# The first two tiles in another order on every queue: mixing tables made from 24 stacked rows, low parts on VectorE, small transfers behind the taps

## The chip, the core and the metric

The kernel runs on one NeuronCore of a Trainium2 chip. The core has five engines with queues of their own: TensorE (PE, matrix products; its weight loads are shown as PEld), VectorE (DVE), ScalarE (ACT), GpSimd (POOL) and SyncE (SP, which here only issues transfers). ACT and POOL issue transfers too. Each queue is worked off in order, and the queues wait for each other through semaphores. The metric is the device time in microseconds (us) of the whole program.

## The reference

Four residual layers over `x`, which is 64 samples x 32 channels x 512 features in float32: `x = x + ffn(cond(x))`. What matters here is the first layer and the small network beside it:

```python
# layer 0: grouped convolution along the features, 9 taps, plus a bias from the condition;
# then a base matrix 512x512 and a mixture of 28 rank-8 experts, 2 of them chosen per row
c0 = conv(x, weight) + (c @ c_weight.T)[:, :, None] + bias
y0 = c0 @ base_W.T + lora(c0, top2(softmax(c0 @ gate_W.T)))
x1 = x + y0
# layers 1, 2, 3: the conditioning is a 32x32 matrix and a bias for each of the 64 samples
h   = gelu(gelu(cond @ W0 + b0) @ W1 + b1)
att = softmax(h @ W2 + b2)                     # 64 x 8
agg_w = einsum('bk,koi->boi', att, weight)     # 64 x 1024, from a table of 8 rows
agg_b = att @ bias_k                           # 64 x 32
cond(x) = agg_w @ x + agg_b
# layer 1 ffn: 8-bit fake quantisation of rows and of w, product 512x512
# layer 2 ffn: silu(x @ Wg) * (x @ Wu) @ Wd;  layer 3 ffn: 3 experts, 2 of them chosen per sample
```

## The kernel before, in words

The 2048 rows are 16 tiles of 128 rows (4 samples each). **Stage one** does layers 0 and 1 tile by tile, **stage two** layer 2 in four groups of four tiles, beside which the conditioning and the router of layer 3 run, and **stage three** the experts of layer 3. No scheduler sets the order: for each engine the program is written out by hand, one function `step(t)` for each tile in each engine's block, and the order of the calls in it is the order of the queue.

To keep float32 accuracy, an operand is split in a high part of type float32r (names in `h`) and the rest, also float32r (names in `l`), and a product is the sum of three: high x high, high x low, low x high. ScalarE makes the high parts, and VectorE or GpSimd subtract for the low ones.

On TensorE a step of stage one is: `router(t)` (L1771, 12 matmuls with `gah`/`gal`: gate logits and the low-rank inputs), `conv(t+1)` (L1705, 9 matmuls), `base(t)` (L1771, 12 matmuls with `w0h`/`w0l`), `positions(t+1)` (L1716, 4 transposes), `hidden(t)` (L1799, 2 transposes), `mix1(t-1)` (L1821, 3 matmuls with `bd1h`/`bd1l`: the conditioning of layer 1), `linear1(t-2)` and `lora(t)` (L1809, 6 matmuls with `lbh`/`lbl`). In the first two steps more is put between: `scores` (L1744), `mixing_weights` (L1751: `att` transposed; L1756: the bias part) and three times `mixed(l)` (L1763 and L1764: the table of layer l, 64 x 1024 from 8 rows of `mixw`, in plain float32), and in step 1 `weights_t` (L1850, 16 transposes of the quantised weight `wq_rows`).

Each `mixed(l)` is copied out of the banks by ScalarE (`aggs`, L896 to L898), stored to DRAM by SP (L364) and read back in another layout as `ag1` (L373) and `bcol` (L374). From `ag1` GpSimd builds the block diagonal `bd1f` (L509, which waits for `d_tab`), ScalarE its high part (L915), GpSimd its low part (L527), and then `mix1` can run.

The preamble, ahead of step 0, loads weights from SP's queue in a written order, and TensorE runs 20 matmuls on a tile of ones (`junk`, L1722), whose result nobody reads.

The granted clock of TensorE has two levels, 1.2 and 2.4 GHz; in the profile's columns they are 0.50 and 1.00.

## Time and profile before

| | us |
|---|---|
| median of 3 runs | 761.42 (760.94 to 766.59) |
| profiled execution, its own time | 761.69 |
| span of the profiled execution | 760.0 |
| busy time of PE / DVE / ACT / POOL | 742.8 / 454.8 / 301.4 / 349.8 |
| mean granted TensorE clock | 0.990 |

The span is the time from the first to the last instruction; 1.69 us of the profiled execution lie outside of it. TensorE is busy for 98% of the span, and the chain that ended last lies on it for 86%. The busy time hides two things: a matmul at half clock counts as busy for twice as long, and a matmul that is there only to set up a table counts like any other. So the first 47 us have to be read piece by piece, which the rows further down do.

### The profile page before, as it was taken

Reading aid. Unit: us, or ns where it says so; the run is one execution under the profiler, and the core shown is the slowest. Engines: PE = TensorE matmul, PEld = TensorE weight load, DVE = VectorE, ACT = ScalarE, POOL = GpSimd, SP = SyncE. Lnnn points to the kernel's source line nnn. Section 1 sums busy time; section 2 is a strip of 40 time slices with the busy share of each in tenths; the row PEclk is TensorE's granted clock in tenths of the full one; section 3 lists DMA queues with packets and bytes.
Section 4 is the critical chain, followed back from the end, with each engine's and each line's share of the span. In section 5 each row is a group of like instructions: output and inputs, shape, how many; then the busy total and the mean of one; then the engine's idle time right before and its main releaser. Section 6 shows DMA issues by size and latency. Waiting matters only on the chain.

```text
span 760.0 us, 11094 instructions
## 1 busy us (share of the span) xinstructions
PE 742.8 (98%) x3588; PEld 598.4 (79%) x3604; DVE 454.8 (60%) x1047; ACT 301.4 (40%) x578; POOL 349.8 (46%) x381
## 2 busy tenths in 40 slices
PE   8999999999899999999999999998999999999997
PEld 5588887776688888888888888877788887888886
DVE  2566776668623244773567445886578788555443
ACT  6444444443532334243434334231454354434331
POOL 2756667766435613120221015868454645554540
PEclk9799999999999999999999999999999999999999
DMA  9447455634132102210211102423512212221200
GB/s 282 78 84 186 163 168 169 185 119 153 43 138 85 54 0 86 110 28 1 84 61 51 29 24 73 168 57 110 182 43 98 84 43 61 67 79 48 70 28 28
DMA packets 45255, 68.82 MB, mean 91 GB/s; under 512 B 21784, under 2 KB 22040, under 8 KB 44936
## 3 DMA queue, kind: packets, MB, share of 16 engines
q1 hardware_dynamic: 35440, 37.87, 17.0%
q0 software_dynamic: 9152, 29.69, 12.7%
q8 instruction: 31, 0.51, 0.3%
q10 hardware_dynamic: 608, 0.55, 0.2%
q14 instruction: 24, 0.20, 0.1%
HBM read 44.94 MB, written 17.66 MB: 82 GB/s over the span
## 4 chain that ended last, share of the span: by engine, by line
PE 86%; DVE 10%; ACT 2%; issue 2%; DVEq 0%; ACTq 0%
PE bank L2101 24%; PE bank L1957 11%; PE bank L2052 11%; PE bank L2084 11%; PE bank L1771 8%; PE bank L1705 4%; PE bank L1809 3%; PE bank L2063 2%; PE bank L1841 1%; DVE junk L1410 1%; PE bank L1977 1%; PE bank L1821 1%; PE bank L1917 1%; PE bank L1722 1%; PE bank L1716 1%
## 5 line engine op out<-in xcount | busy, mean ns | idle before, releaser
L1562 DVE TENSOR_TENSOR sil<-bank,sil 128x512 f32<-128x512 f32 x56 | 38.6, 690 | 98.0 <-PE bank L2101 98.0
L2101 PE MATMUL bank<-th,wgr 128*128 128x512 f32 x224 | 88.8, 396 | 1.9 <-POOL tl L570 1.8
L2101 PE MATMUL bank<-th,wur 128*128 128x512 f32 x224 | 88.0, 393 | 0.0
L2101 PE MATMUL bank<-tl,wgr 128*128 128x512 f32 x224 | 87.8, 392 | 0.0
L2101 PE MATMUL bank<-tl,wur 128*128 128x512 f32 x224 | 87.7, 391 | 0.0
L1957 PE MATMUL bank<-wda,hh 128*128 128x512 f32 x224 | 87.5, 391 | 0.0
L1957 PE MATMUL bank<-wda,hl 128*128 128x512 f32 x224 | 87.2, 389 | 0.0
L2052 PE MATMUL bank<-wda,xch 128*128 (+1 forms) x272 | 84.5, 392 | 1.8 <-DVE xcl L1588 1.8
L1075 ACT ACTIVATE hh<-sil 128x512 fp32r<-128x512 f32 x56 | 35.4, 632 | 116.7 <-DVE sil L1562 116.7
L1067 ACT ACTIVATE sil<-bank 128x512 f32<-128x512 f32 x56 | 33.4, 597 | 96.7 <-PE bank L2101 96.6
L1564 DVE TENSOR_TENSOR hl<-sil,hh 128x512 fp32r<-128x512 f32 x56 | 45.2, 808 | 39.1 <-ACT hh L1075 39.1
L2052 PEld LDWEIGHTS bank<-wda,xch 128*128 128x128 f32 x272 | 50.6, 188 | 12.5 <-issue 2.3
L1602 DVE TENSOR_TENSOR sil<-bank,b1c 128x512 f32<-128x512 f32 x34 | 23.5, 691 | 58.0 <-PE bank L2052 54.0
L2084 PE MATMUL bank<-wgr,hth 128*128 (+1 forms) x136 | 56.1, 412 | 0.0
L2084 PE MATMUL bank<-wgr,htl 128*128 (+1 forms) x136 | 53.3, 392 | 0.0
L2052 PE MATMUL bank<-wda,xcl 128*128 (+1 forms) x136 | 53.1, 390 | 0.0
L2084 PE MATMUL bank<-wur,hth 128*128 (+1 forms) x136 | 53.0, 390 | 0.0
L2101 PEld LDWEIGHTS bank<-th,wgr 128*128 128x128 f32 x224 | 42.2, 188 | 11.9 <-issue 1.8
L793 POOL TENSOR_TENSOR raw<-raw,prod 128x512 f32<-128x512 f32 x32 | 43.0, 1343 | 18.4 <-ACT prod L1141 10.3
L509 POOL TENSOR_TENSOR bdf<-ag,mask 128x128 f32<-128x128 f32 x32 | 15.2, 506 | 77.0 <-PE bank L1917 58.7
L798 POOL DMA_INDIRECT out_dram<-ob,idx x15 | 15.7, 1047 | 75.3 <-DVE ob L1650 75.3
L2101 PEld LDWEIGHTS bank<-th,wur 128*128 128x128 f32 x224 | 42.5, 190 | 9.1
(347 smaller groups left out, 1806.0 us busy)
## 6 DMA issues: line engine op xcount, KB each, us to landing
tap<-in_x_taps_dram SPq DMA_DIRECT2D x16, 260.0 KB, 2.9
xin<-in_x_rows_dram SPq DMA_DIRECT2D x16, 256.0 KB, 2.9
xd<-xo SPq DMA_DIRECT2D x16, 256.0 KB, 3.2
xc<-xd SPq DMA_DIRECT2D x16, 256.0 KB, 3.9
xres<-xd SPq DMA_DIRECT2D x4, 1024.0 KB, 5.5
xd<-xres SPq DMA_DIRECT2D x4, 1024.0 KB, 5.2
tsd<-tf SPq DMA_DIRECT2D x4, 1024.0 KB, 4.4
raw<-in_w_dram POOLq DMA_DIRECT2D x16, 256.0 KB, 3.0
```

The costliest lines, as they stand in the source:

```text
L793: nc.gpsimd.tensor_tensor(xgb[:, t % 2], xgb[:, t % 2], prods[n - first_], ALU.add).then_inc(ch_xb, 1)
L1067: nc.scalar.activation(sil[:, m % 2], p_pre[2 * m % 3][:], ACT.Silu).then_inc(s_sil, 1)
L1075: nc.scalar.activation(hh[:, m % HSLOTS], hf[:, m % 2], ACT.Copy).then_inc(s_hh, 1)
L1562: v.tensor_tensor(hf[:, m % 2], p_pre[(2 * m + 1) % 3][:], sil[:, m % 2], ALU.mult).then_inc(s_hf, 1)
L1564: v.tensor_tensor(hl[:, m % HSLOTS], hf[:, m % 2], hh[:, m % HSLOTS].bitcast(F32), ALU.subtract).then_inc(s_hl, 1)
L1602: v.tensor_tensor(s1[:, p % 2], bank[(p + 1) % 2][:], b1c[:, bass.ds(at, D)] if kind in "AB" else b1c[:, at:at + D], ALU.add).then_inc(s_s ...
L1705: last = mm(p_cv[:].rearrange("p (b n) -> p b n", b=BPT), w, x, start=(n == 0), stop=(n == 3 * SHIFTS - 1))
L1771: last = mm(dst, x[:, k], w[:, k, :], start=(n == 0), stop=(stop and n == 3 * PH - 1), skip_group_check=True)
L1957: last = mm(p_acc[j][:], h[:, m % HSLOTS, j * P:(j + 1) * P], wda[:, m * D:(m + 1) * D], start=(m == 0 and n == 0), stop=(m == MT - 1 and ...
L2052: last = mm(bank[(p + 1) % 2][:], x, y, start=(k == 0 and n == 0), stop=(k == KT - 1 and n == 2))
L2084: last = mm(out_, x, y, start=(begins and k == 0 and n == 0), stop=(ends and k == FT - 1 and n == 2))
L2101: last = mm(p_pre[(2 * m + b) % 3][:], w[:, (m * KT + kt) * P:(m * KT + kt + 1) * P], x[:, kt], start=(kt == 0 and n == 0), stop=(kt == KT ...
```

## The change

All of it concerns the first two tiles and what precedes them; from tile 2 on every engine's `step` issues the same instructions in the same order, apart from SP, whose transfers of the tables and of the scales `swb` sit at other places among the loads.

- **The tables.** `mixw` and `mixb` (8 rows, float32) are gone. The weights and the bias columns of a layer are one table of 8 x 1056 numbers, loaded as 64 rows of 3 x 132 (`mixr`). GpSimd makes its high part `mixh`, VectorE its low part `mixl`, and three transfers from GpSimd's queue stack them into `mix3`: 24 rows, high, low, high. VectorE makes `att3` from the softmax: high, high, low. One float32r matmul over 24 rows then gives the three products at once, and `mixed(l)` is three matmuls of 396, 396 and 264 columns. The separate bias part is gone.
- **Order.** On TensorE `base(0)` comes ahead of `mixing_weights` and waits for each quarter of `w0l` by itself; `mixed(0)` comes behind `positions(1)`, `mixed(1)` and `mixed(2)` on the two sides of `conv(2)`; `weights_t` comes behind `mix1(0)`. The first block of junk has 15 matmuls for 20. ACT, DVE, POOL and SP have written-out orders for tiles 0 and 1 to match.
- **Who does what.** VectorE makes `lbl` and `wq_rows`, which GpSimd made. GpSimd keeps the four multiplications of `w1_raw`.
- **Transfers.** `conv_raw` is loaded from ACT's queue, ahead of its other loads. `bcol` is read behind the four `ag` reads of a table, and `diag_tile(0)` waits for the four alone. `tap(3)` goes ahead of the tables, `tap(4)` and `xin(2)` ahead of the scales, and the broadcast `swb` moves to n = 2 of SP's loop.

```diff
@@ SP
             load_tap(0)
-            sp.dma_start(conv_raw[:], conv_w).then_inc(d_conv, 16)
...
             sp.dma_start(ga_raw[:], l0_ga).then_inc(d_ga, 16)
+            sp.dma_start(mixr[:], mix_w).then_inc(d_mix, 16)
             sp.dma_start(w0_raw[:], l0_w).then_inc(d_w0, 16)
-            sp.dma_start(mixw[:], mix_w).then_inc(d_mix, 16)
-            sp.dma_start(mixb[:], mix_b).then_inc(d_mix, 16)
             load_tap(1)
...
+            load_tap(3)
             store_agg(0)
-            load_tap(3)
             tables(0)
             store_agg(1)
             store_agg(2)
+            load_tap(4)
+            load_xin(2)
             sp.wait_ge(s_sw, 1)
             sp.dma_start(swd.rearrange("k p -> p k"), wsc[:, 1, :], allow_slow_non_contiguous=True).then_inc(d_sw, 16)
-            sp.wait_ge(d_sw, 16)
-            sp.dma_start(swb[:], swd.rearrange("k p -> (k p)").partition_broadcast(P)).then_inc(d_swb, 16)
...
+                if n == 2:
+                    sp.wait_ge(d_sw, 16)
+                    sp.dma_start(swb[:], swd.rearrange("k p -> (k p)").partition_broadcast(P)).then_inc(d_swb, 16)
@@ POOL
             tap_lo(0)
+            def stack_rows(r, part):
+                pool.dma_start(mix3[r * MIX:(r + 1) * MIX].rearrange("k c l n -> k c (l n)"),
+                               part.rearrange("q l n -> q (l n)")).then_inc(d_mst, 16)
+            pool.wait_ge(d_mix, 16)
+            nc.gpsimd.tensor_scalar(mixh[:], mixr[:], 1.0, 1.0, ALU.mult, ALU.mult).then_inc(s_mix, 1)
+            pool.wait_ge(s_mix, 1)
+            stack_rows(0, mixh[:])
+            stack_rows(2, mixh[:])
+            pool.wait_ge(s_mix, 2)
+            stack_rows(1, mixl[:])
             tap_lo(1)
...
@@ DVE
+            w0_lo(0)
+            w0_lo(1)
+            softmax_one()
+            gating(0, None)
+            softmax_two()
+            w0_lo(2)
+            w0_lo(3)
+            gated(0)
+            dve.wait_ge(s_lbs, 1)
+            v.tensor_tensor(lbl[:], lb_raw[:], lbh[:].bitcast(F32), ALU.subtract).then_inc(s_lbs, 1)
+            hidden_lo(0)
+            t0_lo(1)
             weight_scales()
@@ PE
-            keep_busy(20)
+            keep_busy(15)
...
             def mixed(l):
 
+                pe.wait_ge(d_mst, 48)
+                pe.wait_ge(s_atc, 2)
                 if l > 0:
                     pe.wait_ge(s_agc, 3 * l)
-                mm(bank[5][0:BATCH, :], attt[:, l], mixw[:, l, 0:512], start=True, stop=True)
-                mm(bank[6][0:BATCH, :], attt[:, l], mixw[:, l, 512:AGW], start=True, stop=True).then_inc(s_ag, 1)
+                for dst, c0, c1_ in ((bank[5], 0, 3), (bank[6], 3, 6), (bank[4], 6, 8)):
+                    last = mm(dst[0:BATCH, 0:(c1_ - c0) * MIXC].rearrange("b (c n) -> b c n", n=MIXC), attt[:, l],
+                              mix3[:, c0:c1_, l], start=True, stop=True)
+                last.then_inc(s_att, 1)
```

On TensorE in step 0 the order behind `conv(1)` was this (first the program of before, from the transposes of the softmax weights on; `cvf`, `hm` and `hts` are the inputs of `positions`, `hidden` and `lora`):

```order
L1751 MATMUL bank<-ident,att 8x64 [waits s_at]
L1751 MATMUL bank<-ident,att 8x64 x2
L1756 MATMUL bank<-mixb,attt 64x32 [waits s_atc,d_mix]
L1756 MATMUL bank<-mixb,attt 64x32 x2
L1763 MATMUL bank<-mixw,attt 64x512
L1764 MATMUL bank<-mixw,attt 64x512
L1771 MATMUL bank<-w0h,t0h 128x512 [waits s_w0l]
```

and is now, from the last quarter of `base(0)` on:

```order
L1829 MATMUL bank<-w0h,t0h 128x512 [waits s_w0l]
L1829 MATMUL bank<-w0l,t0h 128x512
L1829 MATMUL bank<-w0h,t0l 128x512
L1807 MATMUL bank<-ident,att 24x64 [waits s_at]
L1807 MATMUL bank<-ident,att 24x64 x2
L1772 MATMUL bank<-ident,cvf 128x4x32 [waits s1_t0l,s1_cvs]
L1772 MATMUL bank<-ident,cvf 128x4x32 x3
L1818 MATMUL bank<-mix,attt 64x396 [waits s_atc,d_mst]
L1818 MATMUL bank<-mix,attt 64x396
L1818 MATMUL bank<-mix,attt 64x264
L1855 MATMUL bank<-ident,hm 112x128 [waits s1_hm]
L1865 MATMUL bank<-lbh,hts 128x512 [waits s_lbs,s1_htl]
```

The 12 matmuls of `base(0)` moved ahead of the table work, and one `mixed` stands between `positions(1)` and `hidden(0)`, where before there was one ahead of `base(0)`, one behind it and one behind `hidden(0)`.

On GpSimd the stretch between the low part of tap 0 and the first block diagonal was

```order
L517 TENSOR_TENSOR tapl<-tap,taph 128x520 [waits s1_taph]
L613 TENSOR_TENSOR lbl<-lb_raw,lbh 112x1024 [waits s_lbs]
L618 TENSOR_SCALAR w_raw<-w_raw,wsc 128x512 [waits s_sw]
L620 TENSOR_SCALAR wq_rows<-w_raw 128x512 [waits s_wqr]
L618 TENSOR_SCALAR w_raw<-w_raw,wsc 128x512 [waits s_sw]
L620 TENSOR_SCALAR wq_rows<-w_raw 128x512 [waits s_wqr]
L517 TENSOR_TENSOR tapl<-tap,taph 128x520 [waits s1_taph]
```

(two more pairs of `w_raw` and `wq_rows` follow, then `bd1f`), and is

```order
L621 TENSOR_SCALAR mixh<-mixr 64x396 [waits d_mix]
L617 DMA mix<-mixh 8x8x396 [waits s_mix]
L617 DMA mix<-mixh 8x8x396
L617 DMA mix<-mixl 8x8x396 [waits s_mix]
L525 TENSOR_TENSOR tapl<-tap,taph 128x520 [waits s1_taph]
L525 TENSOR_TENSOR tapl<-tap,taph 128x520 [waits s1_taph,s_lbs]
L632 TENSOR_SCALAR w_raw<-w_raw,wsc 128x512 [waits s_sw]
L632 TENSOR_SCALAR w_raw<-w_raw,wsc 128x512 x3
L530 TENSOR_TENSOR x1l<-x,x1h 128x512 [waits s1_x1h]
L517 TENSOR_TENSOR bd1f<-ag,mask 128x128 [waits d_tab]
```

so that `lbl` and the four `wq_rows` left this queue, and a multiplication and three transfers stand ahead of the low part of tap 1.

On VectorE tile 0 had the softmax, all four `w0l`, the scales of `w1` and then the gating. Now, behind the first two `w0l`, the first half of the softmax and the first part of the gating (which ends with a cast of `ix`), the queue reads (`attm` and `att` belong to the softmax, `gs` to the gating):

```order
L1324 CAST gs<-ix 128x2 [waits ch_gate]
L1237 TENSOR_REDUCE attm<-atte 64x3 [waits s_g1]
L1238 RECIPROCAL attm<-attm 64x3 [waits ch_set]
L1239 TENSOR_TENSOR att<-atte,attm 64x24 [waits ch_set]
L1240 CAST att<-att 64x3x8 [waits ch_set]
L1241 CAST att<-att 64x3x8 [waits ch_set]
L1242 TENSOR_TENSOR att<-att 64x3x8
L1247 TENSOR_TENSOR w0l<-w_raw,w0h 128x512 [waits s_w0s] x2
L1331 TENSOR_SCALAR gs<-gs 128x1 [waits s1_ge]
```

The second half of `w0l` stands behind the whole softmax, which is three operations longer, and behind the first part of the gating.

## Rows read from the trace of the kernel before

**Rows 1.** Chain of waits in order of time, 0 to 54 us: start us, us, what.
```profile
1.52 7.36 PE bank L1722 x20
15.97 1.66 PE bank L1771 x12
...
21.67 0.89 PE bank L1763 x2
...
23.41 4.52 PE bank L1771 x12
...
32.80 1.71 PE bank L1764 x2
34.51 2.86 PE bank L1809 x6
...
44.70 0.89 PE bank L1850 x16
45.59 0.75 PE bank L1821 x3
46.34 1.39 PE bank L1809 x6
47.74 1.41 PE bank L1771 x12
49.15 2.11 PE bank L1705 x9
51.26 2.76 PE bank L1771 x12
...
54.26 0.44 PE bank L1716 x4
```

**Rows 2.** Windows: stretch, length, busy us of PE, PEld, DVE, ACT, POOL, granted clock, DMA.
```profile
22.00:23.00 1.00, 1.00 (x4) 0.23 (x2) 1.00 (x2) 0.00 (x0) 0.95 (x1) 1.00 0.06 16
...
32.00:34.00 2.00, 2.00 (x3) 0.23 (x1) 0.45 (x1) 0.00 (x0) 1.91 (x2) 0.50 0.78 123
56.50:66.65 10.15, 10.08 (x56) 8.09 (x57) 7.08 (x23) 4.76 (x12) 6.59 (x9) 1.00 0.93 187
```

**Rows 3.** Timeline of ACT, DVE and POOL: start us, us, engine, line, operation, tiles.
```profile
5.84 1.28 POOL L517 TENSOR_TENSOR tapl<-tap,taph 128x520 fp32r<-128x520 f32 x1 [3.19 <-ACT taph L839]
6.28 1.26 DVE L1186 TENSOR_TENSOR cvl<-conv_raw,cvh 128x384 fp32r<-128x384 f32 x1 [4.81 <-ACT cvh L860]
...
14.59 0.60 ACT L856 ACTIVATE t0h<-bank 128x512 fp32r<-128x512 f32 x1 [0.19 <-PE bank L1716]
15.09 0.63 ACT L839 ACTIVATE taph<-tap 128x520 fp32r<-128x520 f32 x1
...
19.87 2.48 DVE L1214 TENSOR_TENSOR w0l<-w_raw,w0h 128x512 fp32r<-128x512 f32 x4
...
30.87 0.38 ACT L935 ACTIVATE hts<-bank 112x256 fp32r<-112x256 f32 x1
...
38.67 0.29 ACT L915 ACTIVATE bd1h<-bd1f 128x128 fp32r<-128x128 f32 x1
...
40.09 0.46 POOL L527 TENSOR_TENSOR bd1l<-bd1f,bd1h 128x128 fp32r<-128x128 f32 x1
...
55.89 0.76 POOL L578 DMA_DIRECT2D wda<-in_wd_dram  x1
```

**Rows 4.** DMA issues: name, queue, count, KB each, median us to landing.
```profile
aggd<-aggs SPq DMA_DIRECT2D x3, 264.0 KB, 3.0
ag<-aggd SPq DMA_DIRECT2D x12, 64.0 KB, 2.5
...
b1b<-in_l_b_dram SPq DMA_DIRECT2D x1, 256.0 KB, 12.2
swb<-swd SPq DMA_DIRECT2D x1, 256.0 KB, 6.1
...
swd<-wsc SPq DMA_DIRECT2D x1, 2.0 KB, 8.8
```

More of the change, by code:

```diff
@@ L1006, in step @@
                     diag_hi(0)
-                if t == 0:
-                    mixed(2)
-            for t in range(TILES):
+            act.wait_ge(d_w0, 16)
+            w0_hi(0)
+            w0_hi(1)
+            act.wait_ge(s_at, 1)
+            nc.scalar.activation(atte[:], att[:], ACT.Exp).then_inc(s_g1, 1)
+            gate_exp(0)
+            w0_hi(2)
+            w0_hi(3)
+            act.wait_ge(d_lb, 16)
+            nc.scalar.activation(lbh[:], lb_raw[:], ACT.Copy).then_inc(s_lbs, 1)
+            conv_out(1)
+            act.wait_ge(s_const, 9)
+            nc.scalar.activation(identb[:], ident[:], ACT.Copy).then_inc(s_atc, 1)
+            act.wait_ge(s_att, 1)
+            nc.scalar.activation(attt[:].rearrange("k l b -> k (l b)"), bank[5][0:3 * MIX, 0:COND_LAYERS * BATCH],
+                                 ACT.Copy).then_inc(s_atc, 1)
+            t0_hi(1)
+            tap_hi(2)
+            hidden_hi(0)
+            mixed(0)
+            mixed(1)
+            gate_exp(1)
+            x1_hi(0)
+            conv_out(2)
+            mixed(2)
+            tap_hi(3)
+            t0_hi(2)
+            diag_hi1(0)
+            hidden_hi(1)
+            mixed1(0)
+            for t in range(2, TILES):
                 step(t)
```

208 lines of the change are left out of this document (102 added, 106 removed).

## Prediction
> **What bounds the kernel now.** I read the chain of waits first: through stage one it lies on TensorE piece after piece with hardly a wait between, so what matters is which work TensorE does and at which clock [rows 1]. A steady step lasts 10.15 us, of which it is busy for 10.08, at clock 1.00 [rows 2]. The last matmuls of tile 1 (`lora(1)`, x6) begin at 46.34, and from there on the steps follow each other in that rhythm [rows 1]. The change leaves those steps alone, so its worth is by how much `lora(1)` begins sooner. Three things stretch the first 46 us. The tables: six chain pieces of L1763 and L1764 between 21.67 and 34.51, of 0.89, 0.86, 1.00, 0.87, 1.77 and 1.71 us, 7.10 in all, of which the first and the last are shown [rows 1]. The clock: `base(0)` takes 4.52 for 2.76 us, `lora(0)` 2.86 for 1.39 [rows 1], and the windows show 0.50 at 32 to 34 us, after 1.00 at 22 to 23 [rows 2]; the engine was busy throughout 22 to 23, but with matmuls of 8 rows. And the junk: 7.36 us for 20 [rows 1].
>
> **The change, step by step**, as times at which TensorE gets to its pieces.
>
> *Start.* Five junk matmuls fewer. The last of the 20 run at the full clock: six float32r matmuls of the same 512 columns take 1.39, or 0.23 each [rows 1], and bfloat16 ones hardly less, so this is 1.1 us. Below, nothing is gained if a load is late: the inputs of `conv(0)` need `cvl`, which ends at 6.28 + 1.26 = 7.54 [rows 3], ahead of the new start at about 8.5. All that follows up to `router(0)` hangs on the same chain, so it starts at 15.97 - 1.07 = 14.9.
>
> *Tile 0.* `router(0)` and the scores end at 17.0, `conv(1)` at about 19.1 (2.11) [rows 1]; its low part of the taps is made on GpSimd by 16.0, behind `taph` at 14.0 to 14.7, unless the mixing part of that queue is late. That part is one multiplication and three issues of about 0.76 [rows 3], which end at about 14.5, since the third waits for `mixl`, behind `gal` on VectorE: just in time, and 0.9 us may be lost there before TensorE sees it. `base(0)` can start at 19.1 with two quarters. The other two come late on VectorE: softmax (12 small operations of about 0.2, five of the gating among them) from 17.3 to 20.1, then two `w0l` of 2.48/4 = 0.62 [rows 3], so 20.7 and 21.35. `base(0)` ends at 22.05, about 0.2 us after it would have without that wait. Then TensorE runs out of work: transposes of `att` 0.3, `positions(1)` 0.44 [rows 1], and `lora(0)` hangs on a chain through ScalarE, `t0h` 0.60, `taph` 0.63, `hts` 0.38 [rows 3] and VectorE's low part of 0.4, about 1.95 us with their overlaps, so it starts at 24.95. `mixed(0)` and `hidden(0)` hide in it, and so do `lbl`, which VectorE makes at about 23 to 24.3 with nothing of GpSimd's beside it, and some 1.1 us of idle time are left.
>
> *Tile 1.* `lora(0)` 1.39, `router(1)` 1.41, `mixed(1)`, `conv(2)` 2.11, `mixed(2)`, `base(1)` 2.76, `positions(2)` 0.44 [rows 1]. No row has a `mixed` of 24 rows. The nearest is a float32r matmul of full height: 1056 columns at 0.23 for 512 are 0.47. The far bound is the float32 form, 1.75 a table [rows 1]; the new ones have the type of the first, so I take 0.47. This comes to 34.0. Next `mix1(0)` needs `bd1l`. The read of `ag1`: the copies of `mixed(0)` end at about 25.7, `aggd` lands 3.0 later, the four `ag` are issued within 1.5 and land after 2.5 [rows 4], so at 32.8; before, the last was behind three `bcol`. That is in time. The wait is on ScalarE, where `bd1h` stands behind `t0h` (0.60): 34.6, plus 0.29 and 0.46 on GpSimd [rows 3], 35.35, so TensorE idles for about 1.1 us again. `mix1(0)` 0.75 and `weights_t` 0.89 [rows 1] lead to `lora(1)` at 37.1. VectorE's `wq_rows` must be there at 36.1: GpSimd's multiplications end at about 31, VectorE's four end at about 34.5.
>
> *Sum.* 46.3 - 37.1 = 9.2 us. The transfers that moved cost nothing in it as long as `tap(3)`, now issued at 16, and `tap(4)`, at 34, land within 8 and 7 us; the longest of before took 12.2 at the start, when all loads were under way [rows 4]. `swb` is the tight one: `swd` is issued at 34.9, lands 8.8 later, and `swb` 6.1 after that, at 49.8, when VectorE wants it for tile 0's last product, which comes about when `lora(2)` does, a step after `lora(1)`: 37.1 + 10.15 = 47.3. Nothing of TensorE waits for that product itself, only VectorE's work queued behind it (the sum of tile 2 and the gating of tile 3), which TensorE needs at `hidden(3)`, most of a step later; I take 0.
>
> *The clock.* It went to 0.50 in the first 40 us after TensorE had run on the 8-row matmuls and on transposes, busy as it was [rows 1, 2]. Between the end of `base(0)` at 22.05 and `lora(0)` at 24.95 it will again do only transposes, narrow matmuls and nothing. If the clock falls there, `lora(0)` takes about 2.8 for 1.39 and the gain is 9.2 - 1.4 = 7.8.
>
> *Two rules.* `cvl`, of 384 elements, took 1.26 us when it began inside GpSimd's `tapl`, while `w0l`, of 512, took 0.62 alone [rows 3]. So a low part on VectorE waits for the GpSimd operation under way: `w0l(0)`, ready for at 15.2, starts at 16.0, when `tapl` ends. This is in my times, and it speaks against moving low parts to VectorE; without it the softmax would start 0.2 us sooner and the sum would be 9.4. The Trainium skill has this as a rule ("SBUF — State Buffer", Who interferes with whom): a VectorE instruction with two SBUF inputs and a GpSimd one that reads SBUF exclude each other for the whole instruction. By this rule, with which these rows agree, the change is safe only as long as GpSimd has nothing beside `lbl`.
>
> As to the clock, rows 2 show a fall after a stretch in which the engine was busy for 1.00 of 1.00 us, so being busy is not enough. The Trainium skill ("TensorE: Matmul & The Clock Gate", Part 1: The HAM clock gate) lays the fall to an idle engine. By that rule alone an idle 1.1 us would not bring it about, which is the first rival.
>
> **The forecast**: the clock falls once. 761.42 - 7.8 = 753.6. The profiled execution took 761.69 with a span of 760.0, so its span would become about 752.2, and the median of before lies 0.27 below its time.
>
> **The rivals.**
> - *No fall of the clock.* For it: the 8-row float32 matmuls, the longest weak work of before, are gone, and junk with idle gaps at 12 to 16 us did no harm. Against it: the 2.9 us gap between full-width products. Gain 9.2: 752.2.
> - *More falls, or narrow matmuls that are dear.* If it is also low around the second gap (34.4 to 38), `mix1(0)` and `weights_t` (1.64 us together) take as much again: gain about 6; with `mixed` at the float32 price in two of the three places (2 x 1.3) about 5. So 755.5 to 756.5.
> - *A transfer is late.* `ag` lands 2.5 later than here or `swb` uses up its slack, each worth 1 to 2.5: 755 to 756.
> - *Slower than before: `mix3` is late.* Its three transfers go through GpSimd's queue in the busiest stretch of the loads. If each takes the 12.2 us of the longest load [rows 4] and they follow one another, the third lands at 9.6 + 36.6 = 46, where TensorE wants it at 22.8. `mixed(0)` stands ahead of `hidden(0)`, and so all of TensorE waits, 23 us: about 775. It eats up the gain from a landing at 32 on, and is slower by 1% from 40 on. Against it: the loads of before were in by about 21 us, the three are 101 KB each, and 200 KB of them go off 8 us ahead of the third.
> - *The change doesn't do what it says*: the order of the queues, row by row, shows that it does; I give it nothing.
>
> **How the numbers follow.** Forecast 0.42, no fall 0.33, more falls or dear matmuls 0.12, late transfer 0.09, `mix3` late 0.04. 1% is 7.6 us, which is about what a measurement of this kernel can tell from no change; it lies at 753.8, just above the forecast, so half of the forecast case (0.20) and nearly all of the first rival (0.32) count as faster, the rest as within 1%. Faster 0.52, within 1% 0.44, slower 0.04. The range is 751.3 to 757.5: below, the first rival with 0.9 us of stalls less than I counted; above, the third and fourth; left out are the late `mix3` and the ends of the others.
>
> **What the profile of the changed kernel would show.** `router(0)` at 14.9; `base(0)` in 2.8 to 3.1 us, ending near 22; `lora(0)` near 25, at clock 0.50 in the forecast; `mixed` pieces of about 0.5 on the chain; `mix1(0)` released by `bd1l` near 35.4 (36.8 after a fall); `lora(1)` near 38.5 (37.1 without a fall); steady steps of 10.15 us. The prediction is wrong if the steady step is longer, if TensorE waits for `mix3` or `ag1`, or if VectorE, with `lbl`, `mixl` and `wq_rows` on top, releases `lora(0)` or `hidden(1)` late.

## The result, and the profile after

| | before | changed |
|---|---|---|
| median (us) | 765.75 of 7 runs (760.94 to 767.38), the 3 shown ahead among them | 755.88 of 7 runs (755.2 to 759.35) |
| profiled execution, span (us) | 760.0 | 753.5 |
| ratio | | 0.9906, interval [0.9881, 0.9932] |
| the changed kernel measured again, 12 runs | | 757.19, ratio 0.9942, interval [0.9913, 0.9971] |

The ratios leave disturbed runs out (one of them is a run of 1049 us in e3 below), while the two medians alone would give 0.9871. The changed kernel is 0.6% to 0.9% faster, by less than the forecast's 1.0%. The time lies in the range, 2.3 us above the forecast. The chain of waits of the changed kernel (start us, us, what), from the first transfer to the first steady step:

```profile
2.72 6.61 DMA mb<-in_mlp_b_dram
...
9.38 0.88 PE bank L1786 x6
10.26 3.70 PE bank L1761 x9
...
17.38 1.65 PE bank L1829 x12
...
21.81 2.74 PE bank L1829 x12
...
27.35 1.66 PE bank L1865 x6
...
30.42 0.62 PE bank L1818 x3
31.04 2.34 PE bank L1761 x9
...
38.55 10.05 DMA swd<-wsc
...
48.62 3.71 DMA swb<-swd
...
52.44 0.09 DVE yt L1300
...
61.90 1.39 PE bank L1865 x6
```

L1786 are the small products of the condition, L1761 is `conv`, L1829 `router` and `base`, L1818 `mixed`, L1865 `lora`. These lines answer to [rows 1]. `router(0)` begins at 17.38, not at 14.9 and not even at the 15.97 of before. `mixed(1)` takes 0.62 where the two table products of before took 1.75 and 1.87, and the last pair 3.48 at half clock. `lora(1)` does not lie on this chain; it stands in the timelines of TensorE, of before (first fence) and of the changed kernel (second):

```profile
46.18 0.40 PE L1809 MATMUL bank<-lbh,hts 112*128 112x512 f32 x1
```

```profile
40.49 0.48 PE L1865 MATMUL bank<-lbh,hts 112*128 112x512 f32 x1
```

It begins 5.7 us sooner. (The 46.34 of the prediction is the same matmul in the chain, which starts a piece when the one before it has ended.) Up to `lora(3)` 0.9 us of that is lost again (61.90 against 66.65 in the chains, 4.75 us), behind `swd` and `swb`.

Why the start is late stands in the timeline of TensorE (start us, us, ..., in brackets the idle time before and its releaser) and in the windows (stretch, length, busy us of PE, PEld, DVE, ACT, POOL, granted clock, DMA share, GB/s):

```profile
1.53 5.98 PE L1778 MATMUL bank<-junk 128*128 128x512 bf16 x15 [1.53 <-DVE junk L1206]
8.04 0.43 PE L1783 MATMUL bank<-condt,cw 128*128 128x64 f32 x2 [0.53 <-DMA fs<-in_fside_dram]
9.38 0.88 PE L1786 MATMUL bank<-condt,mw 128*128 128x64 f32 x6 [0.91 <-DMA mb<-in_mlp_b_dram]
```

```profile
8.00:10.00 2.00, 1.06 (x8) 0.92 (x8) 0.00 (x0) 0.31 (x1) 0.00 (x0) 1.00 0.99 308
10.00:12.00 2.00, 2.00 (x8) 1.63 (x8) 0.00 (x0) 1.65 (x3) 1.20 (x2) 0.54 1.02 385
...
61.90:72.05 10.15, 10.08 (x56) 8.09 (x57) 7.08 (x23) 4.75 (x12) 6.43 (x7) 1.00 0.90 208
```

Behind the 15 junk matmuls TensorE waits for two transfers, `fs` (in at 8.0) and `mb` (in at 9.33), and the clock falls right behind, so `conv(0)` takes 3.70 us instead of 2.33. The five matmuls that were taken out would have covered most of this, but `mb` is late by another part of the change, as e2 and e3 below show: `conv_raw` went ahead of it on ScalarE's queue. The steady step is as in [rows 2], 10.15 us with TensorE busy for 10.08.

### The profile page after: what moved, and what is told of

It reads as the page before. It is cut to its first block, busy times and chain, and to the rows that moved or that the text cites. A ratio compares the mean times of both kernels' runs of the same rounds, so it can differ in the third digit from the quotient of the medians.

```text
span 753.5 us, 11073 instructions
## 1 busy us (share of the span) xinstructions
PE 734.6 (97%) x3574; PEld 596.0 (79%) x3590; DVE 459.2 (61%) x1056; ACT 300.9 (40%) x578; POOL 343.1 (46%) x380
## 4 chain that ended last, share of the span: by engine, by line
PE 85%; DVE 8%; DMA 3%; issue 2%; ACT 1%; SPq 0%; ACTq 0%; DVEq 0%
PE bank L2158 26%; PE bank L2014 12%; PE bank L2109 11%; PE bank L2141 11%; PE bank L1829 7%; PE bank L1761 4%; PE bank L1865 3%; PE bank L2120 2%; DVE junk L1466 2%; PE bank L1897 1%; DMA swd<-wsc 1%; PE bank L2034 1%; PE bank L1877 1%; PE bank L1974 1%; DMA mb<-in_mlp_b_dram 1%
## 5 line engine op out<-in xcount | busy, mean ns | idle before, releaser
L1620 DVE TENSOR_TENSOR hl<-sil,hh 128x512 fp32r<-128x512 f32 x56 | 47.2, 844 | 39.1 <-ACT hh L1097 39.1
L804 POOL TENSOR_TENSOR raw<-raw,prod 128x512 f32<-128x512 f32 x32 | 43.2, 1349 | 15.7 <-ACT prod L1163 7.2
L809 POOL DMA_INDIRECT out_dram<-ob,idx x15 | 15.7, 1047 | 74.4 <-DVE ob L1706 74.4
L2158 PEld LDWEIGHTS bank<-tl,wgr 128*128 128x128 f32 x224 | 42.7, 190 | 8.5
```

The lines of the kernel that those rows point to most:

```text
L804: nc.gpsimd.tensor_tensor(xgb[:, t % 2], xgb[:, t % 2], prods[n - first_], ALU.add).then_inc(ch_xb, 1)
L1620: v.tensor_tensor(hl[:, m % HSLOTS], hf[:, m % 2], hh[:, m % HSLOTS].bitcast(F32), ALU.subtract).then_inc(s_hl, 1)
L2158: last = mm(p_pre[(2 * m + b) % 3][:], w[:, (m * KT + kt) * P:(m * KT + kt + 1) * P], x[:, kt], start=(kt == 0 and n == 0), stop=(kt == KT ...
```

## The experiments

All ratios are to the kernel before, run beside each on the same chip. "`mixed(0)` at" and "`lora(3)` at" say when these pieces begin in the run's profile, in us.

| | median us (runs) | ratio [interval] | `mixed(0)` at | `lora(3)` at | span of the profile |
|---|---|---|---|---|---|
| before | | | | 66.65 | 760.0 |
| e1 before again | 759.22 (1) | | | 65.19 | 757.5 |
| changed | 755.88 (7) | 0.9906 [0.9881, 0.9932] | 25.34 | 61.90 | 753.5 |
| e0 changed again | 757.19 (12) | 0.9942 [0.9913, 0.9971] | 24.13 | 66.11 | 758.2 |
| e2 20 junk | 755.52 (6) | 0.9906 [0.9871, 0.9941] | 25.30 | 65.33 | 758.7 |
| e3 taps' weights by SP | 756.58 (12) | 0.9925 [0.9896, 0.9954] | 24.51 | 63.21 | 755.5 |
| e4 both | 755.3 (6) | 0.9915 [0.9884, 0.9947] | 24.18 | 62.09 | 753.3 |
| e10 e4, `mixl` first | 756.59 (12) | 0.9942 [0.9914, 0.9971] | 24.42 | 62.77 | 755.6 |
| e13 e10, second weights after `mixl` | 756.45 (12) | 0.9916 [0.9889, 0.9942] | 24.18 | 61.41 | 752.7 |
| e15 e10, second weights after the stack | 757.97 (9) | 0.9943 [0.9917, 0.9968] | 23.47 | 63.53 | 756.5 |
| e18 e15, tap 2 ahead, `hts` first | 755.81 (12) | 0.9936 [0.9908, 0.9963] | 23.63 | 62.31 | 753.0 |
| e12 `swd` ahead of tap 4 | 757.55 (12) | 0.9933 [0.9906, 0.9961] | 24.43 | 65.21 | 756.6 |
| e5 `swd` ahead of the tables | 763.66 (12) | 1.0042 [1.0016, 1.0067] | 24.99 | 69.09 | 761.5 |
| e16 `swd` by ScalarE | 763.79 (12) | 1.0004 [0.9982, 1.0027] | 25.24 | 69.95 | 763.4 |
| e19 e18, `swd` and `swb` back to back | 758.92 (12) | 0.9988 [0.9963, 1.0013] | 23.24 | 65.68 | 756.6 |
| e9 before, stacked tables alone | 757.75 (12) | 0.9941 [0.9917, 0.9964] | 25.18 | 65.52 | 756.5 |
| e8 low parts back on GpSimd | 762.96 (12) | 0.9999 [0.9984, 1.0015] | 24.68 | 67.61 | 762.7 |
| e11 e10, e5 and ScalarE's swaps | 761.64 (12) | 0.9994 [0.9967, 1.0020] | 24.02 | 68.60 | 761.5 |
| e14 e13, e12 and ScalarE's swaps | 755.79 (12) | 0.9928 [0.9899, 0.9957] | 23.31 | 61.31 | 754.0 |
| e17 e15 and e16 | 763.86 (12) | 1.0011 [0.9992, 1.0030] | 22.92 | 69.63 | 762.1 |

The span of a profile is `lora(3)` plus 690.7 to 693.5 us in every row but that of e8 (695.1). So in a profile what a version is worth is decided in the first 65 us, and up to 3 us of scatter come behind. (e8's profile has two falls of the clock there, in the windows 200 to 220 and 540 to 560; no other has more than one before the last 20 us.)

**The two kernels again.** No edit.

> The kernel before once more, for its profile alone. Its runs lie at 761 and at 766 us, its profile is of the first kind. If this one is near 766, the windows of TensorE's granted clock show where the 5 us are: expected are further stretches at 0.50, in the first 47 us or between 460 and 600 us, where the profiles of before and of the change differ by 1.3 us. If it is near 761, the rows of the first profile repeat.

> The changed kernel itself once more, unchanged, beside three others on one chip, so that differences under 1% can be read against it. Median 755.9 us +-1.5, ratio to before 0.990. In its profile router(0) at 17.4, mixed(0) near 25.3 with the third stack transfer landing at 25.0, lora(3) near 62. If the places at which TensorE's granted clock falls are fixed by the program, this profile shows 0.50 in 10 to 14 us and none in 24 to 34 as the first one did; if they move from execution to execution, the falls and with them lora(3) lie elsewhere by 1 to 2 us.

The start of one program differs from execution to execution. Windows of the two profiles of the kernel before (first and second fence) and of the changed kernel (third and fourth):

```profile
20.00:40.00 20.00, 19.06 (x64) 10.58 (x63) 10.68 (x26) 8.08 (x21) 15.88 (x12) 0.74 0.40 69
```

```profile
20.00:40.00 20.00, 18.65 (x69) 11.83 (x69) 12.53 (x34) 8.46 (x24) 16.61 (x13) 0.83 0.41 76
```

```profile
0.00:20.00 20.00, 16.65 (x71) 10.12 (x73) 6.51 (x10) 10.78 (x21) 6.88 (x19) 0.91 0.93 260
20.00:40.00 20.00, 17.79 (x93) 13.07 (x92) 16.33 (x48) 12.10 (x34) 7.36 (x10) 1.00 0.68 110
```

```profile
0.00:20.00 20.00, 16.16 (x79) 9.99 (x80) 8.06 (x20) 11.94 (x25) 6.88 (x19) 1.00 0.95 264
20.00:40.00 20.00, 17.35 (x98) 12.78 (x97) 15.77 (x40) 11.57 (x31) 8.59 (x11) 1.00 0.69 122
```

The mean clock of these 20 us is 1.00, 0.91, 0.83 or 0.74, so the loss comes in portions of about one size: 0.09 of 20 us is 1.8 us, which I count as one fall, and 3.4 and 5.2 us as two and three. The first 40 us of before contained three in one execution and two in the other; those of the changed kernel one and none. With no fall at the start, `router(0)` of the second profile was at 15.61, and still `lora(3)` came at 66.11. Its chain names two transfers:

```profile
14.41 9.67 DMA mix<-mixl
...
36.99 11.93 DMA swd<-wsc
...
48.93 6.02 DMA swb<-swd
...
55.06 0.09 DVE yt L1300
```

The third stack transfer now holds TensorE, by 0.47 us, and `swb` holds VectorE's `yt` for 5.4 us. Behind that wait the clock fell after all: from `hidden(3)` at 62.48 to `lora(3)` TensorE took 3.63 us, for 2.00 in the first profile, at 0.63 and 0.52 in the windows 62 to 64 and 64 to 66. The first wait was the slower rival's mechanism, in small; the second was taken as 0.

What the ratios measure stands in the mean granted clock of the runs behind them. Beside e0 it was 0.9906 for the kernel before (31 runs) and 0.9958 for the changed one (12). Of 760 us this difference is 4.0 us, and the mean times differ by 3.75 (761.59 and 757.84). Taken at one clock the two kernels hardly differ. Over the 138 runs of the one and the 19 of the other whose clock is on record, wherever both have two or more at one clock, the mean times are 758.6 and 758.0 us (at 0.994), 758.0 and 757.7 (0.995), 757.2 and 757.2 (0.998). So nearly all that the change gained on average is about two falls fewer, each of 1.8 us. Which edit made them fewer is taken up with the parts of the change.

The other runs test these two and the parts of the change.

**An earlier start.** e2, e3, and e4 with both:

```diff
-            keep_busy(15)
+            keep_busy(20)
```

> The changed kernel with 20 junk matmuls ahead of the preamble, as before, for 15. Theory 1 (the clock): conv(0) ran at half clock, 3.70 us, because TensorE had nothing to do for 0.53 and 0.91 us behind the shorter junk; with 20 it is busy until about 8.9, conv(0) takes 2.3, still begins near 10.3 (the load of mb2 lands at 9.3 as before), and router(0) begins near 16.0 for 17.38: 1.4 us less in the whole. Theory 2 (the loads alone): the clock at that place is set by something else, conv(0) stays at 3.7 us, router(0) at 17.4, and the time is that of the changed kernel. Ratio to before: 0.989 by theory 1, 0.9906 by theory 2.

```diff
             load_tap(0)
+            sp.dma_start(conv_raw[:], conv_w).then_inc(d_conv, 16)
...
-            act.dma_start(conv_raw[:], conv_w).then_inc(d_conv, 16)
```

> The changed kernel with the load of conv_raw back on SP's queue behind the first tap, 15 junk matmuls kept. Theory 1 (the loads): the parameters of the small network, issued 0.47 us sooner on ACT's queue, land at about 8 for 9.33, conv(0) begins at 8.8 to 9, and, with only about 0.7 us of idle time in all, at full clock: router(0) near 15.2 to 15.5, 2 us less. If the short idle time is enough for the clock to fall, conv(0) takes 3.7 and router(0) begins near 16.5. Theory 2 (the loads land when the traffic of all loads allows, whatever the queue): mb2 lands at about 9.3 again and nothing changes.

> The changed kernel with both undone: conv_raw on SP's queue and 20 junk matmuls, so that the first 9 us are those of before. Expected by theory 1: conv(0) near 9.5, router(0) near 16.0 as before, lora(1) near 39.1 for 40.49, 1.4 us less than the changed kernel. If it is faster than with 15 junk matmuls and conv_raw on SP, the clock is what the junk buys; if slower by 1, junk was only in the way.

The first products behind the junk, in e2 (first fence) and in e3 (second):

```profile
9.08 0.88 PE L1786 MATMUL bank<-condt,mw 128*128 128x64 f32 x6 [0.51 <-DMA mb<-in_mlp_b_dram]
```

```profile
7.38 0.43 PE L1783 MATMUL bank<-condt,cw 128*128 128x64 f32 x2 [0.64 <-DMA fs<-in_fside_dram]
7.65 0.83 PE L1786 MATMUL bank<-condt,mw 128*128 128x64 f32 x6
```

With 20 junk matmuls TensorE still waits for `mb`; with 15, and `conv_raw` back on SP's queue, it does not. The larger transfer of `mb` landed 6.6 us after its issue in the changed kernel and 6.3 in e2, but 4.6 in e3 and 4.5 in e4 and in the kernel before (5.7 to 6.6 over all profiles behind `conv_raw`, 4.5 to 5.8 over the others), and it is issued 0.5 us later. TensorE waited for `mb` in all seven profiles with `conv_raw` ahead of it on ScalarE's queue and in none of the thirteen others. So the late `mb` comes from the place of `conv_raw`, and the shorter junk only uncovered it, with the smaller wait for `fs`.

The start did move: `router(0)` at 16.2, 14.7 and 15.7, and `conv(0)` ran at the full clock in all three. The 14.7 of e3, 15 junk matmuls and all, is what the forecast said. It was worth nothing, 755.3 to 756.6. TensorE waited for the third transfer of `mix3`, which had landed at 25.3, 24.5 and 24.1.

**What sets the landing of the stack.** e10 makes `mixl` before `gal`, so that the third transfer is issued 3 us sooner:

```diff
+            dve.wait_ge(s_mix, 1)
+            v.tensor_tensor(mixl[:], mixr[:], mixh[:].bitcast(F32), ALU.subtract).then_inc(s_mix, 1)
             dve.wait_ge(s_gas, 1)
             v.tensor_tensor(gal[:], ga_raw[:], gah[:].bitcast(F32), ALU.subtract).then_inc(s_gas, 1)
```

> The changed kernel with 20 junk matmuls and the taps' weights loaded by SP again (as in the run with both), and VectorE makes the low part of the mix rows ahead of that of the gate (mixl before gal). Theory A (what kept the earlier start from paying is the third stack transfer: issued 14.5, landed 24.1, TensorE waited 1.1 us for it and the clock fell after): mixl at 11, third transfer issued at 12.2 to 12.8 and landed by 23, no wait of TensorE for mix, no fall at lora(0), lora(0) at 25.5 and router(1) not over 1.5 us long, lora(3) at 60 to 60.5, median 754.0 (about 1.3 to 2 below the run with both). Theory B (the loads together set when this transfer lands, wherever it is issued: it lands at 24 again): no difference to 755.3. Theory C (the clock falls there anyway, with or without the wait): mixed(0) 1 us sooner, but lora(0) and router(1) again at 0.50 and median 755.0.

e13 and e15 add a wait of SP ahead of the second weights (1 MB) and all loads behind them:

```diff
             load_xin(0)
+            sp.wait_ge(s_mix, 2)      e13
+            sp.wait_ge(d_mst, 48)     e15
             sp.dma_start(w1_raw[:], l1_w).then_inc(d_w1, 16)
```

> The kernel with mixl ahead of gal, and in it SP waits for mixl before it loads the second weights (1 MB, w_raw of layer 1) and what stands behind them (rows of tile 1, b1b, tap 2, the gate's rows). Theory A (the third stack transfer lands at 24 to 25 wherever it is issued between 11.2 and 15.3, because 3 MB of loads asked for ahead of it share the DMA engines with it): with 1.6 MB fewer loads ahead of it, it lands by 20, mixed(0) runs when its turn on TensorE comes (23.3 to 24), no wait and no fall of the clock behind it, lora(0) at 25.0 to 25.6 and router(1) 1.4 us long; the second weights land near 24 to 25 and are wanted at 27; lora(3) at 59.5 to 60.5, median 753.8. Theory B (a transfer of GpSimd's queue takes 10 to 12 us by itself): it still lands at 23 to 24 and nothing is gained. Rival C: tap 2 or the second weights come late and TensorE waits for these instead: median 756 to 758.

> The kernel with mixl ahead of gal, and SP loads the second weights and what stands behind them only when all three stack transfers have landed. Theory A (the stack lands when the loads beside it are over): with 2.4 MB of loads beside it instead of 4 it lands by 16 to 19, TensorE never waits for mix3, mixed(0) at 23.3 to 24. Theory B (it takes 12 us by itself on GpSimd's queue): it lands at 23 to 24 as ever, the second weights at 29 to 31, VectorE's scales and GpSimd's integers (wanted at 27 to 30) are late, and the kernel is as before this edit or slower, 757 to 759. Under A the second weights land at 22 to 25, in time, lora(3) at 60.5 to 61.5 (yt still waits for swb), median 755 to 756.

The transfer in the chains of e10, e13 and e15:

```profile
11.94 12.44 DMA mix<-mixl
```

```profile
11.68 12.46 DMA mix<-mixl
```

```profile
11.59 5.98 DMA mix<-mixl
...
20.01 5.45 DMA tap<-in_x_taps_dram
...
25.49 0.64 ACT taph L852
...
26.91 2.93 PE bank L1866 x6
```

Issued 3 us earlier, it lands at the same time; the loads issued about when it is (e13) count as much as those ahead of it; with these held back until it is in (e15) it takes half as long and lands at 17.6. So Theory A of e15 is shown: the loads beside the stack set its landing. (In e9 below it was issued at 18.15, behind most of them, took 7.0 us, and landed at 25.1 again.) The Trainium skill ("DMA: Bandwidth & Descriptors", Queues, rings and completion order) has each DMA engine take turns between the queues it has work for. By that, 99 KB on a queue of their own should have come through early; here they took 9.6 to 12.8 us as long as the loads went on.

e15 itself gained nothing, since tap 2, which now stands behind the wait, landed at 25.5, and ScalarE, waiting for it, made `hts` late. e18 mends both:

```diff
             load_xin(0)
+            load_tap(2)
+            sp.wait_ge(d_mst, 48)
             sp.dma_start(w1_raw[:], l1_w).then_inc(d_w1, 16)
...
+            hidden_hi(0)
             tap_hi(2)
-            hidden_hi(0)
```

> The kernel whose second weights wait for the stack, with two more moves: SP asks for tap 2 ahead of that wait, and ScalarE runs hidden_hi(0) ahead of tap_hi(2). Theory A (the late tap 2 was the only thing that the held loads cost): stack landed by 19, tap 2 by 20, mixed(0) and lora(0) as TensorE comes to them, 23.5 and 25.0, mix1(0) near 38 and lora(1) at 39.0 to 39.5, against 40.5 in the changed kernel; lora(3) at 60.0 to 61.0 if yt waits for swb 1 us or less. Median 754.5. Theory B (the clock falls behind the wait for hts wherever it stands, or swb is later still, so that the start is given back): lora(3) at 61.5 to 64, median 755.5 to 757.5, no better than the changed kernel.

From `conv(0)` up to `lora(1)` TensorE waited for no transfer of the head; `mixed(0)` came at 23.63 and `lora(0)` at 25.61, where the clock fell (2.27 and 2.34 us for `lora(0)` and `router(1)`); `yt` waited 2.1 us for `swb`; `lora(3)` was at 62.31. That is Theory B, no better than the changed kernel.

**The round trip of the scales.** e5 has `swd` ahead of the tables of layer 0, e12 behind them but ahead of tap 4, e16 on ScalarE's queue, e19 together with `swb`; in e5 and e16 the tables of the later layers also wait for all three stores of `aggd`:

```diff
             store_agg(0)
+            sp.wait_ge(s_sw, 1)                           e5
+            sp.dma_start(swd..., wsc[:, 1, :], ...)       e5
             tables(0)
             store_agg(1)
             store_agg(2)
+            the same two lines                            e12, e19
+            sp.wait_ge(d_sw, 16)                          e19
+            sp.dma_start(swb[:], ...)                     e19
             load_tap(4)
             load_xin(2)
-            sp.wait_ge(s_sw, 1)
-            sp.dma_start(swd..., wsc[:, 1, :], ...)
...
             mixed(0)                                      (ScalarE)
+            act.wait_ge(s_sw, 1)                          e16
+            act.dma_start(swd..., wsc[:, 1, :], ...)      e16
             mixed(1)
```

> The changed kernel with the store of the weight scales (swd<-wsc) and its wait moved on SP ahead of the table loads of layer 0; SP's wait for it there also holds the table loads, and the tables of the later layers wait for all three stores of aggd. Theory A (the scales' round trip costs 0.95 us in the changed kernel: swd issued 38.55, swb landed 52.33, VectorE's scaled_back(0) waited until 52.44): swd is issued near 31, swb, issued where it was if the queue gets there (48.6 or sooner), lands by 48 to 49, the wait is gone, lora(3) at 61.0 instead of 61.9, median 755.0 (0.9 below the changed kernel's). Theory B (the tables of layer 0 now come 1 us later, since both need the same queue, and bd1l with them): mix1(0) and lora(1) are 0.5 to 1 us later and the gain is eaten up, median 755.9. Theory C (the scales were not on the chain): 755.9 with mix1(0) where it was.

> The changed kernel with one line of SP's moved: the store of the weight scales (swd<-wsc) goes ahead of the loads of tap 4 and of the rows of tile 2, but stays behind the tables of layer 0 (ahead of them it held up bd1f by 7 us, and the kernel took 763.7). Theory A (the scales' round trip lies on the chain: VectorE's yt waited for swb until 52.44 in one profile of the changed kernel, until 54.95 in the second): swd issued near 35.5, landed by 45 to 47, swb landed by 49 to 51, yt no longer waits for it, lora(3) at 61.0 or sooner, median 0.9 to 2.5 below the changed kernel's, 754.5. Theory B (the store is slow because of the loads beside it, wherever it stands; or the loads of tap 4 and of the rows now come late): swb again after 52, no difference.

> The changed kernel with the store of the weight scales issued by ScalarE, on its own queue, between mixed(0) and mixed(1), where ScalarE sat idle for 3.2 us; the tables of the later layers wait for all three stores of aggd. Theory A (the scales' round trip is late because SP comes to it at 37 to 38.6; its own slow landing of 10 to 12 us then runs to 48 to 49): swd issued at 30.5, landed by 41, swb issued by SP at 42 to 43.5 and landed by 46 to 48, yt never waits, lora(3) at 60.5 to 61 in a profile without a fall of the clock, median 1 to 2.5 below the changed kernel's, 755. Theory B (512 four-byte pieces slow whatever stands beside them, as when SP issued them ahead of the tables and bd1f came 7 us late): the tables of layer 0 land late again, bd1f after 38, mix1(0) after 41, median 758 to 763.

> The same with the scales' store, the wait for it and the load of swb back to back on SP behind the three stores of aggd, ahead of tap 4 and of the rows of tile 2, and no tables of layer 1 between. Theory A (swb is late because the store shares the engines with tap 4, the rows of tile 2 and tap 5): swd issued at 34.5 to 35.5, landed in 9 us by 44.5, swb landed by 49, yt waits 0, tap 4 landed by 49, lora(3) at 59.5 to 60.5, median 753.5, below both kernels. Theory B (512 pieces of four bytes take 10 us or more by themselves, and tap 4, held back behind them, is then late): conv(4) waits for tapl, lora(4) 1 to 3 us late, median 756 to 758.

The transfers between 28 and 50 us (name, queue, count, KB each, median us to landing) of the changed kernel, of e5 and of e16:

```profile
ag<-aggd SPq DMA_DIRECT2D x6, 64.0 KB, 2.5
...
swd<-wsc SPq DMA_DIRECT2D x1, 2.0 KB, 10.1
```

```profile
ag<-aggd SPq DMA_DIRECT2D x4, 64.0 KB, 11.2
...
swd<-wsc SPq DMA_DIRECT2D x1, 2.0 KB, 10.0
```

```profile
ag<-aggd SPq DMA_DIRECT2D x4, 64.0 KB, 11.0
...
swd<-wsc ACTq DMA_DIRECT2D x1, 2.0 KB, 9.9
```

`swd` moves 2 KB in single 4-byte elements and takes 8.5 to 11.9 us wherever it stands (8.8 and 8.5 in the two profiles of before). Ahead of the tables it makes them wait: `ag` lands after 11 us instead of 2.5, `bd1f` waits for 9.3, and `lora(1)` comes at 47.98, 7.5 us late. Another queue changes nothing in that. The Trainium skill says ("DMA: Bandwidth & Descriptors", Issuing engines are not separate DMA queues) that transfers run on the same 16 DMA engines and interleave, whichever engine issued them. The 11.0 of e16 beside the 11.2 of e5 agrees. e12 has `swd` issued at 36.64, sooner by 0.35 us only than in e0, since the stores of `mixed` ahead of it set its time. In e19 `swb` was in time, and tap 4 behind it was not:

```profile
45.49 0.35 SPq L392
45.89 5.04 DMA tap<-in_x_taps_dram
...
51.50 0.59 ACT qt L925
52.13 1.89 PE bank L1897 x4
```

TensorE waited 4.2 us for `qt`, queued on ScalarE behind the `taph` that waited for tap 4: Theory B, by another engine's queue. Of the four places, the change's own is as good as any.

**The parts of the change.** e9 is the kernel before with the stacked tables alone, e8 the changed kernel with `lbl` and `wq_rows` back on GpSimd:

```diff
+            pool.dma_start(mix3[...], ...)                       e9, x3
-                mm(bank[5][0:BATCH, :], attt[:, l], mixw[:, l, 0:512], start=True, stop=True)
-                mm(bank[6][0:BATCH, :], attt[:, l], mixw[:, l, 512:AGW], start=True, stop=True).then_inc(s_ag, 1)
+                for dst, c0, c1_ in ((bank[5], 0, 3), (bank[6], 3, 6), (bank[4], 6, 8)):
+                    last = mm(..., attt[:, l], mix3[:, c0:c1_, l], start=True, stop=True)
```

> The kernel before with the stacked tables alone: mix rows in two float32r parts on 24 rows, three products a layer of 336 ns instead of two float32 ones of 1.3 us and more and a third product for the biases; the order of the queues and VectorE's share stay as before. Theory A (the tables give 2.0 us on TensorE by themselves, mixed 0.6 us instead of about 1.3 a layer, and the order of the queues gives the rest): median 2 to 2.5 below before, ratio 0.997. Theory B (the tables give nothing while the transfers of the head set the start, or the third stack transfer, issued behind the loads, is late): no difference or 1 us slower. Theory C (the tables make nearly all of it): ratio 0.991.

```diff
-            v.tensor_tensor(lbl[:], lb_raw[:], lbh[:].bitcast(F32), ALU.subtract).then_inc(s_lbs, 1)
+            nc.gpsimd.tensor_tensor(lbl[:], lb_raw[:], lbh[:].bitcast(F32), ALU.subtract).then_inc(s_lbs, 1)
...
-                    weight_integers()
+                nc.gpsimd.tensor_scalar(wq_rows[:, k], w1_raw[:, k], MAGIC, QMAX, ALU.subtract, ALU.min).then_inc(s_wqr, 1)
```

> The changed kernel with the low part of lora_b and the four rounded rows of the second weights back on GpSimd, as before the change; the new order of the queues and the tables stay. Theory A (this part gives little: what VectorE saves GpSimd in the first two tiles hides behind TensorE's queue): bd1f is made by GpSimd up to 1 to 3 us later (it waited 0.7 us for its table), mix1(0) the same or up to 1 us later, weights_t(…) the same, median within 1 us of the changed kernel's. Theory B (the low parts on VectorE are what let bd1l and the integers be ready at 38): mix1(0) at 41 or later and the median 2 to 4 us above the changed kernel's, 759 to 761.

e8 gives the whole gain back. GpSimd's timeline in e8, then in the changed kernel:

```profile
21.52 2.49 POOL L629 TENSOR_TENSOR lbl<-lb_raw,lbh 112x1024 fp32r<-112x1024 f32 x1 [4.48 <-ACT lbh L1014]
...
30.70 1.94 POOL L635 TENSOR_SCALAR wq_rows<-w_raw 128x512 bf16<-128x512 f32 x1
...
42.32 0.40 POOL L517 TENSOR_TENSOR bd1f<-ag,mask 128x128 f32<-128x128 f32 x1
```

```profile
30.61 2.70 POOL L632 TENSOR_SCALAR w_raw<-w_raw,wsc 128x512 f32<-128x512 f32 x4 [2.60 <-DVE wsc L1353]
...
35.26 0.40 POOL L517 TENSOR_TENSOR bd1f<-ag,mask 128x128 f32<-128x128 f32 x1 [0.70 <-DMA ag<-aggd]
```

Four `wq_rows` of 1.94 us (VectorE does all four in 1.47) keep GpSimd from `bd1f` until 42.32, so TensorE idles 5.2 us before `mix1(0)`. e8 takes away the queue's room, not the order, and so the new order only pays together with VectorE's low parts. e9 alone stands at 0.9941, as far as the whole change when it was measured again (0.9942), though its profile is no better at `lora(3)` (65.52) than the second of before (65.19). Each ratio lies in the other's interval. The mean clocks say what the profiles do not: 0.9953 in e9 for 0.9900 in the kernel before beside it, which is 4.0 us of the 4.7 by which their mean times differ, and 0.9899 in e8 for 0.9894. The tables alone come with the whole gain in clock, and e8, with its long wait, has none of it. How the tables bring it about is open.

**Combinations**, of edits shown above (ScalarE's swaps are `hidden_hi(0)` ahead of `tap_hi(2)` and `diag_hi1(0)` ahead of `t0_hi(2)`):

> Everything together: 20 junk matmuls, the taps' weights by SP, mixl before gal, the scales' store ahead of the tables of layer 0, and on ScalarE hidden_hi(0) ahead of tap_hi(2) and diag_hi1(0) ahead of t0_hi(2). If the losses add (start 1.4, scales 0.95, the two idle stretches of TensorE before lora(0) and mix1(0) 0.3 to 0.6 each): lora(3) at 58.5 to 59.5 instead of 61.9, median 752.5 to 753.5, which beats both kernels. If one bound takes the place of another (transfers of the head), lora(3) stays at 60.5 to 61.5 and the median at 754.5 to 755.5.

> The three corrections together: second weights behind mixl, the scales' store ahead of tap 4, and on ScalarE hidden_hi(0) ahead of tap_hi(2) and diag_hi1(0) ahead of t0_hi(2). If the losses add: lora(0) at 24.7, lora(1) at 37.5 to 38.5, lora(3) at 58 to 59, median 752.0 to 753.0, below both kernels. If one bound takes the place of another: lora(3) at 60 to 61.5, median 754.5 to 755.5.

> Both together: stack ahead of the second weights, and the scales' store by ScalarE. If each takes its wait away without a new one: mixed(0) by 24, lora(0) by 25.5, lora(3) at 59 to 60, median 753 to 754, below both kernels. If the store by ScalarE holds up the tables: 758 to 763, as then for that run alone. If the second weights come late: the store comes late with them, lora(3) at 62 or later.

With the early store in them, e11 and e17 gain nothing on the kernel before: e11 is 0.5% better than e5, its store alone, and e17 is level with e16. e14 has `lora(1)` at 38.4, 2.1 us ahead of the changed kernel, and loses it to `yt`, which waits 2.2 us for `swb`: `lora(3)` at 61.31. No version beats the changed kernel by more than the intervals.

## Why the prediction was right and wrong

- **The start: wrong, the step that failed.** "So it starts at 15.97 - 1.07 = 14.9." Measured 17.38: 1.4 later than before, 2.5 later than forecast. I checked `cvl`, not the two small transfers `fs` and `mb`, which land at 8.0 and 9.33, and gave no price to putting `conv_raw` ahead of `mb` on its queue (6.6 us to landing, 4.6 in e3); and the idle time was followed by a fall of the clock that costs `conv(0)` 1.37. The second profile had a wait of 1.33 for `mb` and no fall (15.61). e3, without the move of `conv_raw`, starts at 14.7, and shows with e2 and e4 why even that pays nothing: the stack is in at 24 to 25. With that landing the step was bounded from below, and the prediction had that bound only as a rival from 32 us on.
- **Tile 0 from `router(0)` on: right.** 7.15 us forecast to the end of `base(0)`, measured 24.55 - 17.38 = 7.17. `lora(0)` then comes 2.80 later, forecast 2.90. No wait for `w0l` showed.
- **Tile 1: 1.0 us short.** From `lora(0)` to `lora(1)` 12.15 forecast, 13.14 measured. Counted from start to start in the timeline, the two `mixed` take 0.62 each for 0.47, `conv(2)` 2.32 for 2.11, `lora(0)` with `router(1)` 3.00 for 2.80, `base(1)` 2.87 for 2.76, and `mix1(0)` begins 1.62 behind the end of `positions(2)` for 1.35. The idle time in this is 1.25, forecast 1.1, released by `bd1l` as said.
- **The sum:** 9.2 less 2.5 and 1.0 is 5.7, and 5.7 was measured at `lora(1)`. With the fall that the forecast counts it was to be 7.8.
- **Slips in the working.** The pieces named between `base(0)` and `lora(0)` add up to 2.7, not 2.90, and leave 1.5 us idle, not 1.1 (0.96 measured). Tile 1 adds up to 37.0, not 37.1. The upper end of the range names the third and fourth rival and means the second and third, whose times end at 756.5; the last 1.0 up to 757.5 has no row. The two transfers of `mixh` went off 4 us ahead of the third, not 8. None of these moves the forecast by more than 0.2.
- **`swb` at 0: wrong.** It landed at 52.33, not 49.8, since `swd` was issued at 38.55 (forecast 34.9) behind tap 4 and the rows of tile 2, and VectorE's delay did reach `hidden(3)`: 0.9 us in this profile. In the second, `yt` stood 5.4 us.
- **The clock:** one fall in the first 60 us, as forecast, at another place, `conv(0)` and not `lora(0)`. That it was just one is luck: e2 and e3, much the same kernel, had three and two. And the forecast set one fall against a single profile of before, which had three in its first 40 us; the mean clocks above say that this difference is most of the gain. The reason given for the fall, narrow matmuls and transposes, is not needed: in e9 the 8-row matmuls of the tables are gone, TensorE was busy for 1.57 of the 4 us from 22 to 26, and the clock was at 0.50 from 28 to 30. Nor does idle time decide it alone. These are windows of e0 (first) and e4:

```profile
24.00:26.00 2.00, 1.05 (x5) 0.51 (x5) 0.62 (x3) 1.71 (x5) 0.84 (x1) 1.00 0.03 12
...
28.00:30.00 2.00, 2.00 (x14) 1.57 (x14) 1.90 (x6) 0.18 (x1) 0.62 (x1) 1.00 0.47 106
```

```profile
24.00:26.00 2.00, 1.05 (x5) 0.50 (x5) 0.66 (x2) 1.77 (x5) 0.67 (x1) 1.00 0.06 20
...
28.00:30.00 2.00, 2.00 (x11) 2.00 (x10) 1.84 (x4) 0.00 (x0) 0.57 (x1) 0.50 0.51 108
```

  With the same 1.05 us of work in 24 to 26, one falls and the other does not. The first rival, that idle time of 1.1 us brings no fall, holds for some executions and fails for others. The Trainium skill ("TensorE: Matmul & The Clock Gate", Part 1: The HAM clock gate) lays a fall to an idle engine. The prediction drew from it that idle time of about 1 us would not do. In e4 the longest idle time ahead of the fall was 0.93 us, so there it did; in e9 it was 2.43. In e1, the kernel before again, TensorE was busy for all of 22 to 26 and stood at 0.50 in 24 to 26, with only 1.09 of 2 us busy in 20 to 22. So some idle time stands ahead of each of these falls, but e0 had as much as e4 (0.47 and 0.93 us, for 0.41 and 0.93) and no fall: what decides between them is open.
- **From `lora(3)` to the end:** 4.75 us of gain became 6.5. The difference comes between 463 and 535 us, in a stage that the change does not touch; it stays open. It is of the size by which two profiles of the kernel before differ (760.0 and 757.5).
- **The rule on VectorE's low parts:** right, and more was at stake than 0.2 us. In e8 `g` on VectorE took 1.99 us (0.30 alone) beside GpSimd's `lbl` of 2.49. The prediction weighed the danger for VectorE and gave no price to what GpSimd's queue gains, which e8 puts at the whole change.
- **The chances.** The gain of 5.5 us (761.42 to 755.88), or 0.94% by the ratio, is within 1%, and so is the 0.6% measured again; I had put 0.52 above it, because two terms were taken at their best value, the start and `swb`.

## What to carry to other kernels

Before junk or idle work is taken out ahead of the first real product, list every transfer that this product waits for, the small ones on the second queue too, and what is put ahead of them there: here 6 KB landed 6.6 us after its issue behind `conv_raw`, and 4.6 without it. A step that comes earlier is worth only as much as the latest of its other inputs allows, so follow those that come through DRAM or through another engine's copies (here `mix3`, `swb`, `bd1f`) to the same point in time before the gain is added up. And compare two profiles of the unchanged kernel, and the mean clock of all its runs, before a microsecond is given to a cause.
